# Reciprocals stored ahead of the x loads, repeated-row loads over two slots, and the last batch's spread by 0/1 products

## The reference, cut to what matters

```python
x = x + xattn(layernorm(x), ctx)
x = x + ffn(layernorm(x))

def xattn(x, context):                     # 16 heads of 32 channels
    q = rms_norm(x @ q_w + q_b) * norm_q_w
    k, v = rms_norm(txt @ k_w + k_b) * norm_k_w, txt @ v_w + v_b
    k_img, v_img = the same of the image rows, with their own weights
    out = softmax(q k_img / sqrt(32)) v_img + softmax(q k / sqrt(32)) v
    return out @ o_w + o_b

def ffn(x):                                # 2048 tokens, 32 experts, 4 per token, 80 slots per expert
    idx, w = router(x)                     # sigmoid scores, best 3 of 8 groups, best 4 experts
    out[token] += w * (silu(xe @ Wg) * (xe @ Wu)) @ Wd      # for the slots of each expert
    return out + (silu(x @ sg.T) * (x @ su.T)) @ sd.T       # the shared expert, on all tokens
```

## Time and profile before

| | |
|---|---|
| median of three runs | 1226.6 us (1225.8 to 1226.7) |
| the profiled execution | 1225.96 us, its span 1224.2 us |
| VectorE busy | 822.4 us (67%) |
| ScalarE busy | 648.4 us (53%) |
| POOL busy | 196.9 us (16%) |
| mean granted TensorE clock | 0.981 |

### The profile page before, as it was taken

One profiled execution on the slowest core, in us unless ns is written; L12 is line 12 of the kernel. 1 busy time (PEld: TensorE's weight loads), 2 busy tenths in 40 slices (PEclk: granted clock), 3 DMA queues, 4 the chain that ended last, 5 costly groups with the idle time before them and its releaser, 6 DMA issues. The chain is left out here.

```text
span 1224.2 us, 20716 instructions
## 1 busy us (share of the span) xinstructions
PE 1134.4 (93%) x8420; PEld 407.6 (33%) x8420; DVE 822.4 (67%) x1034; ACT 648.4 (53%) x916; POOL 196.9 (16%) x299
## 2 busy tenths in 40 slices
PE   6999999799999989999998999998789999999996
PEld 2442222344222234422223432222344433333332
DVE  6776778697777878777797877986668953222221
ACT  5558986344998644498864458894121121222221
POOL 1220000143000014300002330001010002333442
PEclk9999999899999989999998999999889999999999
DMA  9751000758200075810016682013933317999842
GB/s 309 176 112 35 2 2 16 183 121 202 57 2 2 30 183 124 206 37 2 2 54 169 136 201 105 2 36 114 308 144 121 129 46 280 364 311 315 252 64 30
DMA packets 143321, 152.46 MB, mean 125 GB/s; under 512 B 108913, under 2 KB 109169, under 8 KB 137969
## 3 DMA queue, kind: packets, MB, share of 16 engines
q1 hardware_dynamic: 135792, 133.93, 37.1%
q0 software_dynamic: 5120, 10.82, 4.6%
q10 hardware_dynamic: 2304, 6.29, 1.9%
HBM read 104.06 MB, written 21.77 MB: 103 GB/s over the span
## 5 line engine op out<-in xcount | busy, mean ns | idle before, releaser
L696 ACT ACTIVATE work<-ps 128x1024 f32<-128x1024 f32 (+1 forms) x416 | 403.1, 1021 | 43.0 <-PE ps L1167 39.3
L1173 PE MATMUL ps<-work,vals 128*32 128x512 f32 (+2 forms) x1664 | 221.0, 603 | 1.8 <-ACT work L696 0.6
L1024 PE MATMUL ps<-wts,work 128*128 128x512 f16 x864 | 194.1, 379 | 2.8 <-DVE work L753 2.4
L1167 PE MATMUL ps<-quer,keys 32*128 32x512 f16 x2496 | 171.8, 377 | 19.8 <-ACT work L696 5.6
L935 DVE TENSOR_TENSOR work<-work 128x2048 f32<-128x2048 f32 x64 | 146.6, 2291 | 6.2 <-ACT work L696 0.7
L935 DVE TENSOR_TENSOR attn<-attn,work 128x2048 f32<-128x2048 f32 x62 | 142.0, 2291 | 5.5 <-ACT work L696 0.7
L1024 PE MATMUL ps<-wts,hl 128*128 128x512 f16 x432 | 107.7, 404 | 25.5 <-DVE hl L753 18.5
L1024 PEld LDWEIGHTS ps<-wts,work 128*128 128x128 f16 x864 | 83.6, 98 | 108.2 <-issue 6.8
L1987 PE MATMUL ps<-wring,xgt 128*80 128x512 f32 x256 | 114.9, 592 | 0.0
L521 POOL TENSOR_SCALAR small<-small 128x1 f32<-128x1 f32 x68 | 18.7, 274 | 570.8 <-ACT work L610 570.8
L1167 PEld LDWEIGHTS ps<-quer,keys 32*128 32x128 f16 x2496 | 46.2, 92 | 189.2 <-ACT work L696 162.8
(11 more groups left out here) (209 smaller groups left out, 1329.6 us busy)
## 6 DMA issues: line engine op xcount, KB each, us to landing
wring<-in_wx SPq DMA_DIRECT2D x32, 1536.0 KB, 9.2
raw<-in_ctx SPq DMA_DIRECT2D x52, 256.0 KB, 3.2
rb<-sums_inverse ACTq DMA_DIRECT2D x48, 128.0 KB, 3.1
work<-in_x SPq DMA_DIRECT2D x4, 1024.0 KB, 6.0
table<-nums SPq DMA_DIRECT2D x16, 256.0 KB, 2.4
work<-in_x SPq DMA_DIRECT2D x12, 256.0 KB, 5.2
x<-work SPq DMA_DIRECT2D x12, 256.0 KB, 2.8
x2t_rows<-nums SPq DMA_DIRECT2D x12, 256.0 KB, 2.7
```

The costliest lines, as they stand in the source:

```text
L696: act.activation(prob[0:rows, s % PROBS, 2 * half:2 * half + 2, :], ps[0:rows, 2 * pair:2 * pair + 2, :], ACT.Exp, scale=SCALE).then_inc(a ...
L1024: mm = pe.matmul(out, lhs(a, c)[:, cols], wts[:, w, z, c * D:(c + 1) * D], start=(k == 0), stop=(k == len(steps) - 1))
L1167: mm = pe.matmul(ps[:, 2 * pair + h % 2, :], k[h * HD:(h + 1) * HD, :], q[h * HD:(h + 1) * HD, :], start=(e == 0), stop=(e == len(terms) - 1))
L1173: return pe.matmul(ps[h * HD:(h + 1) * HD, NUM, :], vals[a:z, ORDER[n], g * P + h * HD:g * P + (h + 1) * HD], prob[a:z, s % PROBS, h, :], ...
```

## The change

- Seams: `store_sums` stands at the start of slot 1, before the slot's context load; `load_x` and the two residual loads come after that context load. The DRAM buffer has one part for each stored batch.
- ScalarE issues the four loads of group 0 in slot 1, and the four of group 1 in slot 2, after that slot's `key_high`.
- The last batch's reciprocals are not stored. POOL builds eight tiles `sel` of 128x128 float32 from columns of the identity: entry (k, m) is 1 where k is the row of m's head for group g and kind t. TensorE multiplies `sel` by `rcp`, so that each head's reciprocal is repeated on its 32 partitions of a PSUM bank, and VectorE weighs from there.
- Group 0's two products stand ahead of the flag, after one gate product (gate 0). Groups 1 to 3 are the first work of TensorE in the second program. Up 0 and gate and up 1 follow; gate and up 2 stand before the last transpose, 3 after the last router products. VectorE and ScalarE orders are changed to match.
- SyncE loads expert 2 with the first ones, expert 3 after the last selection product.

```diff
+SEL_BANK = [(4, 5), (1, 3), (6, 7), (4, 5)]
+GATE_BANK, FLAG_BANK = 0, 2
@@ SyncE, projection
-                    if b > 0:
-                        load_x(bb, b)
                     for i in range(SLOTS):
+                        if b > 0 and i == 1:
+                            store_sums(bb - 1)
...
-                        if i == 0 and b > 0:
+                        if i == 1 and b > 0:
+                            load_x(bb, b)
                             residual(q, b - 1, 0)
                             residual(q, b - 1, 1)
-                        if i == 1 and b > 0:
-                            store_sums(bb - 1)
...
                 last_loads(p, bb)
-                store_sums(bb)
-                sp.wait_ge(s_rd, 16 * (bb + 1))
@@ POOL, after its last projection
+                pool.wait_ge(a_at, gn(out_batch(bb - 1), NG - 1))
+                for g in range(NG):
+                    for k in range(2):
+                        pick = ident[:, 2 * g + k:P:HD].unsqueeze(2).to_broadcast([P, 4, HD])
+                        ins = pool.tensor_copy(sel[:, g, k, :].rearrange("p (h r) -> p h r", h=4), pick)
+                ins.then_inc(s_const, 1)
@@ ScalarE, projection
                         spread(bb, 0)
+                    if b > 0 and i == 2:
                         spread(bb, 1)
@@ TensorE, end of the last batch
                     pe.wait_ge(f_wlo, 3 * p + 1)
-                    gate(SG, 0, 0)
-                    pe.wait_ge(f_wlo, 3 * p + 2)
-                    gate(SU, 0, 2).then_inc(s_gate, 1)
-                    gate(SG, 1, 1)
+                    for k, (c, a, z) in enumerate(steps):
+                        pe.matmul(ps[:, GATE_BANK, :], swt[SG][:, a, c * D:c * D + P], m.x2t[0][:, :, z, c, :],
+                                  start=(k == 0), stop=(k == len(steps) - 1))
+                    pe.wait_ge(s_const, 6 + p)
+                    pe.wait_ge(a_rcp, bb + 1)
+                    for t, bank in ((1, SEL_BANK[0][0]), (0, SEL_BANK[0][1])):
+                        pe.matmul(ps[:, bank, :], sel[:, 0, t, :], rcp[:, :], start=True, stop=True)
...
             one_pass(0)
-            pe.wait_ge(a_nt, gn(B - 1, NG - 1))
             pe.wait_ge(f_chk, 2 * B + 2)
@@ second program, SyncE
-            spread(0)
             sp.dma_start(rraw[:, :], d["rw"]).then_inc(s_xl, 16)
-            spread(1)
             sp.dma_start(ebias[:, :], d["ebias"].partition_broadcast(P)).then_inc(s_xl, 16)
-            for n in (0, 1, 4, 5):
+            for n in (0, 1, 2, 4, 5):
                 load_expert(n)
-            sp.wait_ge(t_at, NG)
-            load_expert(2)
+            sp.wait_ge(t_sel, NG - 1)
             load_expert(3)
@@ second program, VectorE
-                dve.wait_ge(s_rl[g // 2], 64)
+                image, text = SEL_BANK[g]
+                upto(dve, t_sel, g)
-                TT(nums[:, g, 1, :], nums[:, g, 1, :], rbl[:, g, 1, :], ALU.mult).then_inc(link, 1)
-                TT(nums[:, g, 0, :], nums[:, g, 0, :], rbl[:, g, 0, :], ALU.mult).then_inc(t_mt, 1)
+                TT(nums[:, g, 1, :], nums[:, g, 1, :], ps[:, image, :], ALU.mult).then_inc(link, 1)
+                TT(nums[:, g, 0, :], nums[:, g, 0, :], ps[:, text, :], ALU.mult).then_inc(t_mt, 1)
@@ second program, VectorE's order: gates 0 and 1 after the weighing; gate 2 after norm_low(3),
@@ its low part and gate 3 among the first steps of the router's choice
@@ second program, TensorE
+            def spread(g):
+                image, text = SEL_BANK[g]
+                if g == 3:
+                    pe.wait_ge(t_mt, 1)
+                pe.matmul(ps[:, image, :], sel[:, g, 1, :], rcp[:, :], start=True, stop=True)
+                pe.matmul(ps[:, text, :], sel[:, g, 0, :], rcp[:, :], start=True, stop=True).then_inc(t_sel, 1)
...
+            for g in range(1, NG):
+                spread(g)
+            gate_up(0)
+            pe.wait_ge(t_mt, 2)
             gate_up(1)
-            gate_up(2)
-            gate_up(3)
             for j in range(QT):
                 output(j)
...
             for j in range(QT - 1):
                 turn_out(j)
+            gate_up(2)
             turn_out(QT - 1)
             for j in range(3 * QT, NT):
                 rt_last = route(j)
             rt_last.then_inc(e_r, 1)
+            gate_up(3)
             gate_up(4)
             down_first(0)
```

More of the change, by code:

```diff
@@ L157, in __init__, with attention_program @@
         self.yf = [at(f"yf{i}", o * KB_, [CAP, D], F32) for i, o in enumerate((108, 110, 60, 62))]
-def attention_program(nc, m, d, x1_dram, x2_dram, r_dram, table, out, s_turned, s_xr, s_gate):
+def attention_program(nc, m, d, x1_dram, x2_dram, r_dram, table, out, s_turned, s_xr):
     with ExitStack() as ctx:
@@ L623, in spread @@
                 for h in range(4):
[L624 removed]
+                    rows = r_dram[out_batch(bb - 1)][h * HD + 2 * g:h * HD + 2 * g + 2, :].rearrange("r q -> (r q)")
                     act.dma_start(rb[h * HD:(h + 1) * HD, g % 2, :, :].rearrange("p t q -> p (t q)"),
@@ L1266, in attention @@
                     pe.wait_ge(f_wlo, 3 * p + 1)
-                    gate(SG, 0, 0)
-                    pe.wait_ge(f_wlo, 3 * p + 2)
-                    gate(SU, 0, 2).then_inc(s_gate, 1)
-                    gate(SG, 1, 1)
[L1272 to L1277, removed]
+                    steps = [(c, a, z) for c in range(NC) for a, z in PARTS]
+                    for k, (c, a, z) in enumerate(steps):
[5 more added lines that the diff above has]
+                        pe.matmul(ps[:, bank, :], sel[:, 0, t, :], rcp[:, :], start=True, stop=True)
             def one_pass(p):
@@ L1320, in lay_attention, with ffn_program @@
     }
-def ffn_program(nc, m, d, x1_dram, table, r_dram, out, s_turned, s_gate):
+def ffn_program(nc, m, d, x1_dram, table, out, s_turned):
     with ExitStack() as ctx:
@@ L1355, in ffn_program @@
         s_const, s_i0 = event("s_const"), event("s_i0")
-        s_rl = [event(f"s_rl{i}") for i in range(2)]
         r_lo = event("r_lo")
-        t_mt, t_at, t_hi, t_lo = (event(n) for n in ("t_mt", "t_at", "t_hi", "t_lo"))
+        t_sel, t_mt, t_at, t_hi, t_lo = (event(n) for n in ("t_sel", "t_mt", "t_at", "t_hi", "t_lo"))
         t_mm, t_out = event("t_mm"), event("t_out")
@@ L1524, in norm_store @@
                          ps[:, TURN_BANK[j], :].bitcast(F16)).then_inc(n_out, 1)
+            for g in range(NG):
+                out_high(g)
             gate_tanh(0)
             gate_high(0)
-            out_high(0)
             gate_tanh(1)
-            out_high(1)
             gate_high(1)
-            out_high(2)
-            out_high(3)
+            for j in range(QT):
+                norm_high(j)
+            for j in range(QT - 1):
+                norm_store(j)
             gate_tanh(2)
+            norm_store(QT - 1)
             gate_high(2)
-            norm_high(0)
-            norm_high(1)
-            gate_tanh(3)
-            norm_high(2)
-            norm_high(3)
-            gate_high(3)
-            for j in range(QT):
-                norm_store(j)
             act.wait_ge(e_r, 1)
@@ L1546, in _ @@
                            scale=-1.0 / WS).then_inc(e_ez, 1)
-            for n in range(4, 13):
+            for n in range(3, 13):
                 gate_tanh(n)
@@ L1686, in _ @@
             dve.memset(ia[:, :], 0.0).then_inc(s_const, 1)
-            gate(0)
             weigh(0)
-            gate_low(0)
             weigh(1)
-            gate(1)
             out_low(0)
@@ L1701, in _ @@
             out_low(3)
-            gate(2)
-            gate_low(2)
+            gate(0)
+            gate_low(0)
+            gate(1)
             out_rows(0)
+            gate_low(1)
             out_norm(0)
@@ L1708, in _ @@
             out_norm(1)
-            gate(3)
             out_rows(2)
@@ L1715, in _ @@
             out_norm(3)
-            gate_low(3)
             norm_low(3)
+            gate(2)
             dve.wait_ge(s_const, N_CONST)
@@ L1883, in gate_up @@
                 upto(pe, f_h, n - 1)
-                for w, bank in ((SG, n % 2), (SU, 2 + n % 2))[1 if n == 1 else 0:]:
+                for w, bank in ((SG, n % 2), (SU, 2 + n % 2))[1 if n == 0 else 0:]:
                     mm = product(ps[:, bank, :], lambda a, c: swt[w][:, a, c * D + it * P:c * D + (it + 1) * P],
@@ L2043, in build @@
         s_xr = ctx.enter_context(nc.semaphore("s_xr"))
-        s_gate = ctx.enter_context(nc.semaphore("s_gate"))
-        attention_program(nc, m, d, x1_dram, x2_dram, r_dram, table, out, s_turned, s_xr, s_gate)
-        ffn_program(nc, m, d, x1_dram, table, r_dram, out, s_turned, s_gate)
+        attention_program(nc, m, d, x1_dram, x2_dram, r_dram, table, out, s_turned, s_xr)
+        ffn_program(nc, m, d, x1_dram, table, out, s_turned)
 def kernel(**inputs):
```

36 lines of the change are left out of this document (14 added, 22 removed).

## The result

Over 11 runs of each, the changed kernel has a median of 1222.6 us (1218.9 to 1224.7) and the kernel before 1226.7 us (1224.5 to 1232.8). The medians are 4.1 us apart, and the ratio is 0.9959, with a 95% interval of 0.9946 to 0.9972: 0.4% faster. The forecast was 1205.5 us with a range from 1198 to 1214, so the sign was right and the size was wrong. The profiled run of the changed kernel took 1218.86 us and is the fastest of its 11.

A forecast was written before the change was run, and what follows sets the result against it. TensorE, busy 93% of the span, was taken as the bound, with time to gain only where it stands or runs at lower clock. Gains 13.7 + 2.9 + 4.2 = 20.8 us gave 1205.5 us, range 1198 to 1214.

The forecast's parts named there:

- part one: The three batch seams: reordered store and loads let TensorE gain 5.4, 4.7 and 3.6 us, in all 13.7.
- Store's landing: At the seams: the reciprocals' store, issued ahead of x and residual rows, lands in 3.0 us instead of 5.8, 5.4 and 4.9.
- Four issues: At each seam: four load issues instead of eight before ScalarE's square, half of 3.90 us, so 1.9 us less.
- TensorE's stop near 1 us: At the seams: TensorE's 5.89 us stop at 221.6 shrinks to about 1 us and its clock stays at 2.4 GHz.
- VectorE the limit at key 7: At the seams: key 7's context cast limits TensorE's gain to VectorE's advance plus slack: 5.4, 4.7 and 3.6 us.
- the hand-over: From the last batch's reciprocal to the second program's second down product: 7.1 us earlier, 2.9 before the start and 4.2 after.
- The flag: End of the last batch: the flag's product moves from 853.32 to about 850.4, and the second program starts 2.9 us earlier.
- The head: Start of the second program to its second down product: 4.2 us gained by filled gaps and fewer returns at lower clock.
- (a): At the seams: the store's landing stays near 5 us and only four issues are saved, 1213 us; chance 0.2.
- (b): At the seams: VectorE does not limit slots 3 to 7, so TensorE regains 21 us, 1198 us; chance 0.12.
- (c): Second program's start gains nothing, since gate 2 stands before the transpose the router waits on: 1209.4 us; chance 0.12.
- (d): Second program's start: TensorE goes on at 1.2 GHz, so the kernel is slower, up to 1244 us; chance 0.04.

The follow-up runs named there:

- the kernel whose loads are out of the way: Changed kernel with x issued at its old place ahead of the reciprocals and both residual tiles only in slot 4: 1206.5 us, ratio 0.9841 to the kernel before.
- seams alone: Kernel before with only the seam edits (store first, x and residual rows behind it, repeated-row loads over two slots): 1231.8 us, ratio 1.0055.
- old order, two slots: Changed kernel with x, residual rows and store in the old order, repeated-row loads still over two slots: 1213.4 us, ratio 0.9894 to the kernel before.
- the two orders with the tile ahead of them: Changed kernel with slot 2's context tile issued ahead of x and residual rows (1226.4 us), or behind those but ahead of the first key transpose (1213.8 us).
- the kernel with the tile ahead of the transposes: Changed kernel with slot 2's context tile issued behind x and residual rows but ahead of the first key transpose: 1213.8 us, ratio 0.9907 to the kernel before.
- the kernel with eight loads in slot 1: Changed kernel with all eight repeated-row loads in slot 1 again: 1230.7 us, ratio 1.0056 to the kernel before.

## Why the prediction was wrong in size

**The step that failed** is the last paragraph of part one: "The context tile for ScalarE's slot 2 is issued at the old time, 219.35, behind 1.75 MB; needed at 225.6. It is covered by about 1.5 us; if not, VectorE's advance shrinks by what is missing." It was issued at 221.37, because the first transpose started 0.5 us later and held SyncE's queue 2.73 us instead of 1.24, and took 8.6 us to land, so it was there at 229.97: 4.4 us late where I had 1.5 to spare. The rule of that paragraph held: of VectorE's 5.8 us at key 3, the 0.6 us for the issues of slot 2 and ScalarE's wait of 5.10 us leave 0.1, and 0.02 was measured (230.62 for 230.64). My landing of 6 us for x was read from traffic as it was; x took 7.0, and the residual rows behind it 8.8. The paragraph named the consequence and put no chance on it, the sum took the whole 13.7 us, and none of the four rivals was this one. Only the last sentence, on what would show it wrong, named the tile.

I had asked what the store is behind, and not what the queue does while it waits for the reciprocal. In those 3.4 us x had been crossing (345 GB/s from 214 to 216). Moving the store to the front turns them into an idle hole and puts 1.5 MB into the one stretch where tile, transposes and repeated rows are all due.

**The seams by their terms.** Store's landing 3.0: 2.0 measured. (The 5.8 before stood behind 1.75 MB and not 1.5: a context tile is issued at 213.56, between residual rows and store.) Four issues, 1.95: 1.93. TensorE's stop near 1 us: 0.17. VectorE the limit at key 7: in the kernel whose loads are out of the way, key 7 starts 5.2 us earlier for a forecast of 5.4. There the three seams give 1217.0 − 1206.5 = 10.6 us, both of one set, where 13.7 stood in the sum. In the kernel that I predicted they give a loss: 6.1 us alone on the kernel before, 8.7 − 4.1 = 4.6 beside the hand-over. From 13.7 to −4.6 it is 18.3 us, more than the whole error of 20.8 − 4.1 = 16.7; the rest came back at the hand-over.

In the profiles a seam's loss or gain follows from how late VectorE stands at key 4, and where the tile is late, from the tile. The table has two intervals, both from the start of a reciprocal, for the three seams in turn: to VectorE's low half of key 4, which needs that tile, and to the next reciprocal. The other rows are differences from the first, minus for earlier.

| kernel | to the low half of key 4 | to the next reciprocal |
|---|---|---|
| before | 18.52, 17.88, 17.50 | 213.08, 212.10, 207.78 |
| seams alone | +3.4, +3.2, +1.3 | +2.7, +2.8, +1.3 |
| the change | +0.1, +1.3, +1.0 | −0.6, +1.0, +1.1 |
| old order, two slots | −1.5, −0.3, −1.5 | −2.3, −0.6, −1.5 |
| x early, residual rows late | −4.0, −3.1, −3.6 | −4.7, −3.5, −4.2 |

The last row stands beside the forecast 5.4, 4.7 and 3.6 for a kernel whose tile is not late: 12.4 in all for 13.7.

**The flag**, 2.9: its product stands 5.39 us after the start of the reciprocal and stood 8.25 after it, 2.86 gained. It starts the second program 5.67 us later, 5.60 before.

**The head**, 4.2: the second down product comes 53.50 us after the start where it came 59.27, 5.8 gained. The selection product was 0.86 at full clock as taken from the earlier trace rows. The granted clock is 0.50 from 857.5 to 859.3, 0.57 from there to 861.1 and 1.00 after that, so it was back after at most 3.6 us where I took 5.3, and the outputs start 14.6 us after the start for a forecast of 15.7. It then stays at 1.00 to 1200, where before it was at 0.50 again from 875 to 878 and from 899 to 908. The second down product starts at 911.03 for a forecast of 911.1, though the start came 1.5 us later than I had it (857.53 for 856.0). Hand-over in all: 8.56 in the profile and 8.7 in the runs, for a forecast of 7.1. That the start of the second down product was met to 0.1 us is luck: the start of the program 1.5 us too late and the head 1.6 us too short cancel.

**The rivals.** (a) did not happen: 1.75 MB right behind the store, and it landed in 2.0 us. The page of the Trainium skill that spoke for it ("DMA: Bandwidth & Descriptors", "Latency and other measured facts") gives 2 us of HBM access latency at high load. This store does not test that: from 216.2 to 216.9 the DMA engines move 0.23 MB, about its own 256 KB, and the issue of x begins only at 216.32, so it was nearly through before the traffic behind it ran. I had taken the page as a warning on the store; the transfers behind it were what grew. (b) did not: with the loads out of the way VectorE was the limit at key 7. (c) did not, the head gave more than its term. (d) did not, the clock rose.

**What stays open.** Why 16 DMA engines with a share over 1 move only 217 to 256 GB/s from 224 to 232, with a transpose landing in 8.6 or 14.6 us that took 4.1 before. The packets give a hint. Here are those of the changed kernel from 219 to 222 and from 224 to 228:

```profile
DMA packets 534, 1.10 MB, mean 365 GB/s; under 512 B 16, under 2 KB 16, under 8 KB 534
DMA packets 1411, 1.02 MB, mean 256 GB/s; under 512 B 1129, under 2 KB 1129, under 8 KB 1411
```

In the kernel before, 1078 of 1218 packets from 219 to 222 are under 512 B, at 188 GB/s, while one transpose is under way. So the low rate goes with many small packets, and these with the transposes; that they slow the tile was not tested, since no kernel left them out. The runs show that it matters when the large loads cross and in which order tile and transposes stand, and that repetition of rows does not. Nor do they say why the same tile lands so differently, after 8.6 us in the changed kernel's first seam and 11.2 in that of the seams alone. By the table above that difference is where the seams' loss of 6.1 us on the kernel before, 4.6 beside the hand-over and 1.4 in the profiled run would come from. That run is 3.8 us below the median of its kernel, and no profile of a median run was taken.

## What to carry to other kernels

When a small urgent transfer is put ahead of large ones, look at what the queue does while the urgent one is not ready yet. If the large ones filled that hole, leave there what fits (x here) and move what is not urgent (the residual rows) several slots behind, not right behind. Then read the next item in each queue as if the first stop were gone, its issue time and its landing under the new load: here the tile, and after mending it the transposes. A cover of 1.5 us on a landing of some 5 us, read from calmer traffic, is no cover and deserves a rival with a chance of its own.

## What the runs showed of the hardware

A DMA transpose holds the queue that issues it: 1.24 us on SyncE in the first seam of the kernel before (the line below), 2.73 in the changed kernel, 5.24 beside eight repeated-row loads, and 7.63 and 9.41 us for two in the two orders with the tile ahead of them. It delays all that SyncE issues behind.

```profile
218.07 1.24 SPq L369 DMA_TRANSPOSE keys<-work  x1
```

A store of 256 KB landed in 2.0 us with nothing ahead and 1.75 MB right behind, 2.5 with a 1 MB load 3.4 us ahead, and 5.8 behind 1.75 MB.

Repeated-row loads of 128 KB whose outermost dimension is 2 instead of 16, of the same rows, cost the whole kernel some 70 us (1292.8 for 1224.6).

How long TensorE stood does not alone tell whether its clock falls. It kept the clock over stops of 1.36, 2.49, 2.53 and 2.64 us (the next 12 products took 2.75 us), and came back at the lower clock from stops of 1.97, 1.98, 2.66, 2.76, 3.06 and 4.27 us (the next 12 took 4.22 to 5.08, the next 24 after 1.97 us took 7.03). The first row is of the kernel with the tile ahead of the transposes, second seam, where a stop of 1.61 us had come 7.3 us earlier; the other two are of the kernel with eight loads in slot 1, first and third seam:

```profile
447.99 7.03 PE L1030 MATMUL ps<-wts,work 128*128 128x512 f16 x24 [1.97 <-DVE work L759]
224.80 4.36 PE L1027 MATMUL ps<-wts,hl 128*128 128x512 f16 x12 [3.06 <-DVE hl L756]
661.57 4.22 PE L1027 MATMUL ps<-wts,hl 128*128 128x512 f16 x12 [1.98 <-DVE hl L756]
```
